# Two attention layers' sums: the maxima of four groups fetched by one transfer per head and turned by one TensorE product

## The reference, cut to what matters

```python
def _gatv2_layer(x, src, dst, Wl, bl, Wr, br, att, bias, heads, out_ch, concat):
    xl = (x @ Wl + bl).reshape(N, heads, out_ch)
    xr = (x @ Wr + br).reshape(N, heads, out_ch)
    e = jax.nn.leaky_relu(xl[src] + xr[dst], NEG_SLOPE)
    logits = jnp.einsum('ehc,hc->eh', e, att)
    m = jax.ops.segment_max(logits, dst, num_segments=N)
    ex = jnp.exp(logits - m[dst])
    denom = jax.ops.segment_sum(ex, dst, num_segments=N)
    alpha = ex / denom[dst]
    msg = xl[src] * alpha[..., None]
    out = jax.ops.segment_sum(msg, dst, num_segments=N)
    ...
```

## Time and profile before

| | |
|---|---|
| median of three runs | 6667.94 us (6659.76 to 6667.99) |
| the profiled execution, its own time | 6665.56 us |
| its span, from the first to the last instruction | 6663.1 us |
| mean granted TensorE clock over the span | 0.758 |
| busy: TensorE, VectorE, ScalarE, GpSimd | 4832.1, 4076.8, 2301.7, 4523.2 us |
| sums of layer 1: first transfer issued, first transfer of what follows | 1405.05, 1882.81 us |
| sums of layer 2: the same | 3109.92, 3521.74 us |

### The profile page before, as it was taken

One profiled execution on the slowest core, in us unless ns is written; L12 is line 12 of the kernel. 1 busy time (PEld: TensorE's weight loads), 2 busy tenths in 40 slices (PEclk: granted clock), 3 DMA queues, 4 the chain that ended last, 5 costly groups with the idle time before them and its releaser, 6 DMA issues. The chain is left out here.

```text
span 6663.1 us, 98108 instructions
## 1 busy us (share of the span) xinstructions
PE 4832.1 (73%) x22735; PEld 3486.0 (52%) x22735; DVE 4076.8 (61%) x13068; ACT 2301.7 (35%) x5676; POOL 4523.2 (68%) x4354
## 2 busy tenths in 40 slices
PE   3677775347776666544886996666666799999999
PEld 2344443236664444333776995555555455555555
DVE  7998985589976766335887445444444644344343
ACT  4344444369943333334994003222222400000000
POOL 1777777678867777777887661777777177276473
PEclk8555555579965555556997998877777799999999
DMA  5988865556644444333444884655555299899998
GB/s 202 296 300 289 280 192 148 133 101 142 140 81 108 105 108 102 81 80 57 76 76 127 286 289 135 185 159 160 159 161 153 75 303 305 290 305 300 307 305 258
DMA packets 915215, 1226.12 MB, mean 184 GB/s; under 512 B 248092, under 2 KB 652720, under 8 KB 901674
## 3 DMA queue, kind: packets, MB, share of 16 engines
q1 hardware_dynamic: 593614, 879.21, 41.2%
q0 software_dynamic: 206208, 217.12, 16.7%
q10 hardware_dynamic: 114828, 123.48, 5.6%
HBM read 981.30 MB, written 239.21 MB: 183 GB/s over the span
## 5 line engine op out<-in xcount | busy, mean ns | idle before, releaser
L1180 POOL DMA_INDIRECT ACC<-table,TABS x1760 | 1665.4, 946 | 623.1 <-issue 623.1
L1495 POOL DMA_INDIRECT BUF<-table,TABS x840 | 796.3, 948 | 589.1 <-issue 245.7
L1261 POOL DMA_INDIRECT adjacency<-TABS x600 | 962.8, 1605 | 251.2 <-issue 221.8
L1801 POOL DMA_INDIRECT TABS<-table,SPOT_SRC x836 | 789.1, 944 | 317.9 <-issue 317.9
L1983 PE MATMUL picked<-BUF,G 128*128 x2368 | 595.4, 433 | 445.8 <-DVE ACC L2008 401.3
L1983 PEld LDWEIGHTS picked<-BUF,G 128*128 128x128 f32 x2368 | 525.6, 327 | 687.3 <-issue 687.3
L2379 PE MATMUL asum<-BUF 128*128 128x144 f32 x3520 | 561.0, 305 | 165.7 <-DVE BUF L2357 162.7
L1991 DVE TENSOR_TENSOR picked<-picked,ACC 128x512 f32<-128x512 f32 (+1 forms) x440 | 247.7, 563 | 573.4 <-DMA ACC<-table,TABS 517.0
L1824 PE MATMUL pre<-wmat,BUF 128*128 128x128 f32 x1672 | 320.7, 352 | 370.5 <-DVE BUF L1850 357.6
L2379 PEld LDWEIGHTS asum<-BUF 128*128 128x128 f32 x3520 | 476.2, 197 | 196.7 <-issue 186.3
L2325 ACT ACTIVATE BUF<-iota_row,TABS 128x128 f32<-128x128 f32 x1760 | 555.1, 386 | 22.5 <-PEq L98 22.5
(11 more groups left out here) (449 smaller groups left out, 9763.6 us busy)
## 6 DMA issues: line engine op xcount, KB each, us to landing
TABS<-adjacency SPq DMA_DIRECT2D x272, 512.0 KB
BUF<-in_edge_pair SPq DMA_DIRECT2D x836, 128.0 KB
BUF<-adjacency SPq DMA_DIRECT2D x102, 1024.0 KB
BUF<-adjacency SPq DMA_DIRECT2D x204, 512.0 KB
adjacency<-zeros ACTq DMA_DIRECT2D x44, 1792.0 KB
G<-adjacency SPq DMA_DIRECT2D x136, 512.0 KB
kept<-ACC SPq DMA_DIRECT2D x220, 272.0 KB, 3.8
G<-kept SPq DMA_DIRECT2D x220, 272.0 KB
```

What stands on the lines that cost most here:

```text
L1180: po.indirect_dma_start(rows[:, slot, j, 0:width], None, tab, bass.IndirectOffsetOnAxis(ap=SRC[:, q * GT + j:q * GT + j + 1], axis=0)).the ...
L1261: po.indirect_dma_start(adj_flat, bass.IndirectOffsetOnAxis(ap=PLACE[:, k:k + 1], axis=0), TOTAL[:, k:k + 1], None, compute_op=ALU.add).th ...
L1495: po.indirect_dma_start(R[:, q % deep_ring, j, :], None, table, bass.IndirectOffsetOnAxis(ap=SRC[:, k:k + 1], axis=0)).then_inc(S(f"gather ...
L1801: po.indirect_dma_start(R[:, g % RD, j, :], None, table, bass.IndirectOffsetOnAxis(ap=SPOT_SRC[:, k:k + 1], axis=0)).then_inc(S(f"gathered ...
```

## The change

In both layers the maxima of the four groups of a turn (16 tiles) are fetched together in the turn's first step: one DMA per head, of 16 rows of 512 bytes. `MX` has two rooms for turns, in place of four for groups, and holds 16 H rows (128 with H = 8, 16 with H = 1). One product per turn turns them into 16 H columns of `mcol`. `less_max` and `first_max` read their group's part of `mcol` (`max_of`); with H = 8 the heads of a tile then lie 16 elements apart, where they lay side by side.

```diff
-            MX = BUF[2][0:TH, at:at + RING, :]
+            MX = BUF[2][0:RING * TH, at:at + 2, :]
...
-            by_group = head_d[0:H * TILES * P].rearrange("(h g t e) -> g t h e", h=H, t=GT, e=P)
+            of_four = head_d[0:H * TILES * P].rearrange("(h n k e) -> n h k e", h=H, k=RING * GT, e=P)
...
                 def fetch_max(q, slot, turn):
-                    wait(sp, S("mcol"), q - RING + 1)
+                    if slot:
+                        return
+                    wait(sp, S("mcol"), turn - 1)
                     settle(sp, "sync")
-                    if H == 1:
-                        sp.dma_start(MX[:, slot, :], by_group[q, :, 0, :]).then_inc(S(f"max{slot}"), 16)
-                    else:
-                        for t in range(GT):
-                            sp.dma_start(MX[t * H:(t + 1) * H, slot, :], by_group[q, t]).then_inc(S(f"max{slot}"), 16)
+                    for h in range(H):
+                        sp.dma_start(MX[h * RING * GT:(h + 1) * RING * GT, turn % 2, :], of_four[turn, h]
+                                     ).then_inc(S(f"max{turn % 2}"), 16)
...
                 def turn_max(q, slot, turn):
-                    pe.wait_ge(S(f"max{slot}"), 16 * (1 if H == 1 else GT) * (turn + 1))
-                    wait(pe, S("mfirst"), q - 1)
-                    m = pe.matmul(mcol[slot % 2][:, 0:TH], MX[:, slot, :], ident[0:TH, 0:TH], start=True, stop=True)
-                    m.then_inc(S("mcol"), 1)
+                    if slot:
+                        return
+                    pe.wait_ge(S(f"max{turn % 2}"), 16 * H * (turn // 2 + 1))
+                    wait(pe, S("mfirst"), RING * (turn - 1))
+                    pe.matmul(mcol[turn % 2][:, 0:RING * TH], MX[:, turn % 2, :], ident[0:RING * TH, 0:RING * TH],
+                              start=True, stop=True).then_inc(S("mcol"), 1)
+
+                def max_of(slot, turn):
+                    return mcol[turn % 2][:, 0:RING * TH].rearrange("p (h r t) -> p r t h", h=H, r=RING)[:, slot]
...
                 def less_max(q, slot, turn):
-                    ve.wait_ge(S("mcol"), q + 1)
+                    ve.wait_ge(S("mcol"), turn + 1)
                     ve.wait_ge(S(f"got{slot}"), 16 * (turn + 1))
-                    ve.tensor_tensor(DIF[:, slot], by_head(LOGIT[:, slot, :]), by_head(mcol[slot % 2][:, 0:TH]),
+                    ve.tensor_tensor(DIF[:, slot], by_head(LOGIT[:, slot, :]), max_of(slot, turn),
                                      ALU.subtract).then_inc(S("dif"), 1)
```

More of the change, by code:

```diff
@@ L2340, in less_max @@
                 def less_max(q, slot, turn):
-                    ve.wait_ge(S("mcol"), q + 1)
+                    ve.wait_ge(S("mcol"), turn + 1)
                     ve.wait_ge(S(f"got{slot}"), 16 * (turn + 1))
-                    ve.tensor_tensor(DIF[:, slot], by_head(LOGIT[:, slot, :]), by_head(mcol[slot % 2][:, 0:TH]),
+                    ve.tensor_tensor(DIF[:, slot], by_head(LOGIT[:, slot, :]), max_of(slot, turn),
                                      ALU.subtract).then_inc(S("dif"), 1)
                 def first_max(q, slot, turn):
-                    ve.tensor_tensor(RHS[:, slot, :, W + H:W + 2 * H], by_head(mcol[slot % 2][:, 0:TH]),
+                    ve.tensor_tensor(RHS[:, slot, :, W + H:W + 2 * H], max_of(slot, turn),
                                      NEWSEG[:, bass.ds(q * GT, GT)].unsqueeze(2).broadcast_to([P, GT, H]), ALU.mult
```

## The result

The changed kernel takes 6710.9 us (median of 4 runs, 6709.64 to 6711.93) against 6667.97 (4 runs, 6659.76 to 6670.44): a ratio of 1.0066, with a 95% interval of 1.0053 to 1.0078. It is slower by 43 us. The profiled execution took 6709.64 us, its span is 6707.8.

A forecast was written before the change was run, and what follows sets the result against it. VectorE was taken to bound layer 1 (2.01 us a group) and ScalarE layer 2. Terms -8 (TensorE) + 7 (clock) + 7 (queue) + 0 = +6 us on 6665.6 gave 6671.6, plus 2.4 to the median: 6674, range 6657 to 6710.

The forecast's parts named there:

- rival 2: SP queue, layer 1: slower because eight transfers have a pitch over 0.34 us; at 0.47, 6717 us; chance 0.18.
- the forecast: Whole kernel: nothing that can be measured, as three terms nearly cancel; 6674 us, chance 0.60.
- The pitch of the eight transfers: SP queue, layer 1: issue pitch of 16-row transfers, taken as 0.33 us, with 0.47 as the high bound.
- the threshold: SP queue, layer 1: above a pitch of 0.34 us the typical landing of rows is too late as well.
- The queue's cost, given the pitch: SP queue, layer 1: every fourth row fetch goes out 1.2 us late, slow landings stall VectorE 14 x 0.5: +7 us.
- TensorE, -8 us: Layer 1: 220 turning products become 55, shortening VectorE's waits for sums at half clock and the cold start: -8 us.
- The cap: End of layer 1: GpSimd's last scatter ends at 1873.9, so the stage could end only 8.2 us earlier.
- The clock, +7 us: TensorE, layer 1: longer pauses raise half clock from 45 to 90 us, each us costing 0.15: +7 us.
- Rival 3: TensorE, layer 1: fewer products let the clock fall to half for half of the stage; 6694 us, chance 0.09.
- The strided read, 0: VectorE, layer 1: `less_max` and `first_max` reading numbers 16 apart take 0.02 us more, inside the adds' pitch: 0.
- rival 4: VectorE, layer 1: slower if strided `less_max` and `first_max` took twice their 0.18 us; 44 us, 6718, chance 0.05.
- ScalarE and layer 2, 0: ScalarE's work stays the same; in layer 2 the savings are covered by ScalarE at 100%: 0.

The follow-up runs named there:

- six and two: The changed kernel with six of a turn's eight small transfers in its first step and two in its second: 6668.6 us, ratio 0.9999 to before.
- two groups in a row: Kernel before with one product per turn; 8-row transfers of two groups stand together, eight in every second step: 6680.99 us, ratio 1.0012 to before.
- product alone: Kernel before with one product per turn; maxima still fetched by four 8-row transfers per step, a turn ahead: 6668.06 us, ratio 0.9997 to before.
- product per group: The changed kernel's fetches, but a product of all 128 columns made again for every group: 6716.65 us, ratio 1.0072 to before.
- two heads per step: The changed kernel with its eight transfers spread two per step, a turn ahead: 6668.91 us, ratio 1.0001 to before.

## Why the prediction was wrong

What happened is rival 2, at 0.18; the forecast was no change, at 0.60. By steps:

- **The pitch of the eight transfers.** This is the step that failed. The prediction had two rows for it, 0.33 from transfers of 8 and 32 shorter rows and 0.47 from transfers of 16 rows of 7 KB. It took 0.33 "as these rows are nearest in size". The measured pitch is 0.45 (eight in 3.62 us; median of one 420 ns), so for 16 rows the price is nearly that of the earlier trace rows, though those rows are 14 times as long. The prediction had named a pitch of 0.36 or more as the sign that it is wrong. Here the rows that agreed in the number of rows were the ones to go by, and bytes made little difference. On SP's own queue, transfers of 512-byte rows measured 288 ns for 8 rows (median), 420 for 16 and 599 for 128. Why 16 rows cost more than 8 stays open: the number of rows alone doesn't set it, for 32 short rows took 308 ns on ScalarE's queue, and no run changes rows, bytes and shape one at a time. That the threshold was put at 0.34, right beside the chosen 0.33, should have moved the chances as well: the likeliest case rested on a hundredth of a microsecond.
- **The queue's cost, given the pitch.** Right in mechanism and nearly in size. At 0.47 rival 2 had the fetch 2.3 us late and a stall of 1.0 in 55 turns, 57 us; measured are 2.36 us and 0.78 per turn, 43 us with everything else in it. The landing of 2.8 us held (2.9 at 1618.83), and the slack, put at 1.3, comes out between 1.1 and 1.6. The waits for rows grew by only 31.4 us, 0.57 per turn, because in the other turns VectorE was held up by TensorE at half clock instead. And at the lateness that the sum had assumed, 1.2 us, the forecast's term was +7 us: with six and two, 55 times late by that, VectorE's waits for rows are 8.1 us in all; with two groups in a row, 110 times, they are 9.5 and the kernel loses 8. So the term was about right for the pitch that it was given.
- **TensorE, -8 us.** The mechanism is right: with the product alone the waits for sums fall by 8.2 us and the last add comes 9.3 earlier. The cap was mis-sized. It was taken as 8.2 us, from a scatter that ended at 1873.9. This end moved with the change, to 1879.8 (5.9 us), and what follows starts 3.0 us after the last scatter in place of 0.7 after the last add (another 2.3). Together that is about the 8.2. Without stalls the product per turn is worth about nothing here (0.9988 to 1.0006), and 7.7 us where GpSimd has a group less.
- **The clock, +7 us.** Half clock was expected to grow from 45 to 90 us. With a mean of 0.87 over 497 us it is 2 x 0.13 x 497 = 129. Each us of it costs 21.7 / 129 = 0.17 of waiting for sums, close to the 0.15 of the prediction. So this term, 84 us more at 0.17, is some 14 us in place of 7 (an estimate). But its cause lies with the stalls: the four kernels that turn a whole turn at once and have no late fetch show 0.98 to 0.99, above the 0.94 of before. **Rival 3**, that fewer products lower the clock, is refuted as the cause of the loss. So is, for this stage, the risk that was read there out of the Trainium skill (TensorE: Matmul & The Clock Gate, "What's actually happening"), as an objection to taking work from TensorE: 330 fewer matmul records in a stage left the clock higher. More half clock came with more waiting of TensorE: 0.87 with a fetch late by 2.15 us in each turn, 0.70 with one late by 4.0. With the fetches late as in the changed kernel the extra products do go with a higher clock (product per group, 0.91 against 0.87), but not with a shorter time. Why the small products of before go with 0.94 isn't settled. No run separates their number from the pauses around them.
- **The strided read, 0.** Right. `less_max` and `first_max` take 181 and 184 ns on average in the changed kernel, 180 and 181 where the 32 columns lie side by side (product alone), and 180 and 181 in the kernel with two heads per step as well, which has the strided read and no loss. So rival 4 is refuted. By the rule on lines of 8 bytes in the Trainium skill (SBUF — State Buffer, "Door 1: The DMA port swizzle") each step to a new line should have cost a penalty; for these 32 numbers the trace shows at most 3 ns.
- **ScalarE and layer 2, 0.** Right: 411.7 us and ScalarE at 100%.

With the pitch of the earlier trace rows the sum would have been the 6717 of rival 2, off by 6 us. That it comes so near is partly luck: rival 2's sum leaves out the prediction's own +7 for the clock, with which it is 6724, and takes a gain of 8 that the runs without a late fetch don't show.

## What to carry to other kernels

Moving transfers together on a queue that also carries the loop's main fetch can make that fetch late. Multiply the number of transfers in a row by the measured issue time of transfers of the same shape, take off the room that the queue has between two fetches, and compare what is left with the slack, which is the time from the fetch's issue to its use, less its landing. Where no transfer of that shape is in the trace and the bounds lie on both sides of the threshold, the issue time is what to measure first. Fewer transfers are no gain by themselves if the queue had room; spread over the steps, or as one transfer, the same fetch cost nothing. And where two engines end a stage a few microseconds apart, a gain on the one shows only when work of the other is taken out too.

## What was not expected of the hardware

- The issue of one transfer of 128 rows took 599 ns, against 8 x 0.45 = 3.6 us for the same 128 rows in eight: here the cost grew with the number of transfers far more than with their rows.
- A scatter of GpSimd took 1631 to 1639 ns on average in three kernels whose loop ran without stalls, and 1611 to 1612 before and in the changed kernel. The speed of the loop alone doesn't explain it: with a product per group the loop is as slow as in the changed kernel, and a scatter took 1626 ns. The cause wasn't tried. It is small for one, but 244 of them took back 4 to 6 us of an 8 us gain.
- TensorE's granted clock rose from 0.94 to between 0.98 and 0.99 of full over the middle of the stage when three of four small products were taken out and nothing was late.
